# Zero rows only in the unused slots of a row buffer, and the places of rows worked out during the first batch of attention

## The reference

```python
# 1: attention, 16 heads, Dh = 32. Masked scores are zero, not minus infinity
scores = einsum('bthd,bshd->bhts', x @ Wq, x @ Wk) * tril(ones(T, T))
attn = softmax(scores / T ** 0.5, axis=-1)
x = layernorm(x + einsum('bhts,bshd->bthd', attn, x @ Wv) @ Wo)

# 2: routing over 4 experts by token id; ctx_2048[e] serves as Wg, Wu and Wd
expert = min(clip(token_ids, 0, 24999) // 6250, 3)
for e in range(4):
    y = (silu(x @ W[e].T) * (x @ W[e].T)) @ W[e].T
    out = where(expert == e, y, out)
x = layernorm(x + out)

# 3: gated feed-forward, of each 4 neighbours in h only the 2 largest are kept
h = silu(x @ w_gate) * (x @ w_up)
x = layernorm(x + sparsify_2to4(h) @ w_down)
```

## Time and profile before

| | us |
|---|---|
| median of 3 runs | 1153.69 |
| the profiled execution | 1154.83 |
| its span, first to last instruction | 1153.0 |
| TensorE busy in it | 1046.8 (91%) |
| VectorE busy | 749.7 (65%) |
| ScalarE busy | 479.6 (42%) |
| GpSimd busy | 278.7 (24%) |
| mean granted TensorE clock | 0.980 of full |

### The profile page before, as it was taken

One profiled execution on the slowest core, in us unless ns is written; L12 is line 12 of the kernel. 1 busy time (PEld: TensorE's weight loads), 2 busy tenths in 40 slices (PEclk: granted clock), 3 DMA queues, 4 the chain that ended last, 5 costly groups with the idle time before them and its releaser, 6 DMA issues.

```text
span 1153.0 us, 18006 instructions
## 1 busy us (share of the span) xinstructions
PE 1046.8 (91%) x6022; PEld 846.7 (73%) x6023; DVE 749.7 (65%) x1756; ACT 479.6 (42%) x882; POOL 278.7 (24%) x479
## 2 busy tenths in 40 slices
PE   2888999898999977499999999999999999999994
PEld 1666777776777766388788888888888888888873
DVE  4668768868886897365664845664565546654666
ACT  4268648856874895122333322221121222222113
POOL 1017444733653453122221002400000000000222
PEclk9999999999999998799999999999999999999997
DMA  5797725754672590122444101410010101100001
GB/s 182 187 303 214 188 87 153 198 128 143 176 196 55 147 274 11 64 84 81 149 164 165 37 1 22 53 38 1 1 44 29 36 0 36 37 1 1 38 37 73
DMA packets 56223, 110.37 MB, mean 96 GB/s; under 512 B 6032, under 2 KB 6032, under 8 KB 56144
## 3 DMA queue, kind: packets, MB, share of 16 engines
q1 hardware_dynamic: 51504, 95.97, 29.6%
q0 software_dynamic: 4640, 13.39, 3.1%
HBM read 72.11 MB, written 35.14 MB: 93 GB/s over the span
## 4 chain that ended last, share of the span: by engine, by line
PE 56%; DVE 2%; ACT 0%; issue 0%; POOLq 0%; POOL 0%; ACTq 0%; DVEq 0%
PE f_bank L42 54%; PE f_bank L1388 1%; PE f_bank L1380 1%; PE f_bank L1430 1%; DVE rows_kept L1727 0%; DVE ln_stats L813 0%; DVE big_hi L1108 0%; DVE hs_lo L1715 0%; DVE ln_mv L815 0%; ACT L826 0%; POOLq L1174 0%; DVE h L1705 0%; ACT hs_hi L1557 0%; POOL out L1342 0%; DVE ln_shift L833 0%
## 5 line engine op out<-in xcount | busy, mean ns | idle before, releaser
L1666 DVE TENSOR_TENSOR h<-f_bank,fsg 128x512 f32<-128x512 f32 x64 | 44.2, 691 | 181.9 <-PE f_bank L42 181.8
L1534 ACT ACTIVATE fsg<-f_bank 128x512 f32<-128x512 f32 x64 | 38.3, 599 | 298.4 <-PE f_bank L42 298.3
L404 PE MATMUL bank<-ident,probs 128*128 128x128 f32 x640 | 109.5, 286 | 37.9 <-DVE pt_lo L674 18.6
L654 DVE CUSTOM_DVE_ANT_0 bank<-bank,mask 128x384 f32<-128x384 f32 (+3 forms) x256 | 123.1, 503 | 24.3 <-PE bank L393 23.9
L531 ACT ACTIVATE probs<-bank,nmax 128x384 f32<-128x384 f32 (+3 forms) x256 | 129.7, 539 | 18.3 <-DVE nmax L665 16.4
L674 DVE TENSOR_TENSOR pt_lo<-bank,pt_hi 128x512 f16<-128x512 f32 (+1 forms) x192 | 114.7, 597 | 20.4 <-ACT pt_hi L541 20.0
L42 PE MATMUL bank<-x_hi,w_qk 128*128 128x512 f32 x256 | 104.9, 418 | 23.0 <-DVE x_lo L679 22.6
L844 POOL TENSOR_SCALAR ln_var<-ln_mv 128x1 f32<-128x1 f32 x43 | 10.0, 232 | 464.1 <-DVE ln_mv L815 464.1
L541 ACT ACTIVATE pt_hi<-bank 128x512 f16<-128x512 f32 (+1 forms) x192 | 102.9, 536 | 35.1 <-PE bank L404 34.3
L404 PEld LDWEIGHTS bank<-ident,probs 128*128 128x128 f32 x640 | 67.4, 141 | 49.2 <-ACT probs L531 28.1
L42 PE MATMUL f_bank<-wd_hi,hs_hi 128*128 128x512 f32 x256 | 100.3, 392 | 3.2 <-DVE rows_kept L1727 3.2
(11 more groups left out here) (225 smaller groups left out, 2438.5 us busy)
## 6 DMA issues: line engine op xcount, KB each, us to landing
big_lo<-q_hi_dram SPq DMA_DIRECT2D x32, 256.0 KB, 3.9
big_lo<-q_lo_dram SPq DMA_DIRECT2D x32, 256.0 KB, 4.7
big_lo<-k_hi_dram SPq DMA_DIRECT2D x32, 256.0 KB, 3.8
big_lo<-k_lo_dram SPq DMA_DIRECT2D x32, 256.0 KB, 5.2
sorted_dram<-z SPq DMA_DIRECT2D x1, 4864.0 KB, 18.7
rows<-sorted_dram SPq DMA_DIRECT2D x19, 256.0 KB, 2.6
x_raw<-x_t SPq DMA_DIRECT2D x4, 1024.0 KB, 9.9
q_hi_dram<-q_hi SPq DMA_DIRECT2D x16, 256.0 KB, 2.3
```

The source lines that it names most:

```text
L404: ins = pe.transpose(TP[u % TR][:, j * P:(j + 1) * P], probs[u % RP][:, j * P:(j + 1) * P], ident[:, :])
L654: dve.tensor_tensor_reduce(out=S[u % SR][:, at:at + cols(r)], in0=S[u % SR][:, at:at + cols(r)], in1=mask[:, T - cols(r):T], scale=1.0, sc ...
L1534: act.activation(fsg[v % 2][:, :], GB[v % 2][:, :], ACT.Silu).then_inc(s_sg, 1)
L1666: dve.tensor_tensor(h[r % 2][:, j, :], UB[v % 2][:, :], fsg[v % 2][:, :], ALU.mult).then_inc(s_h, 1)
```

## The change

The DMA that zeroes the whole row buffer goes, with its semaphores. In its place GpSimd scatters a tile of zeros (`z[0]`) three times, 128 rows each, to the 384 unused slots, after its `norm_heads` of group m = 2 in batch 0. `add_x` of batch 0 waits for these three. The numbers of the unused slots are worked out by 8 new VectorE instructions inside `Route.places` (one sum, three products and three sums, and the cast to `pad_idx`), and `places` now runs in batch 0 at every unit from 1 on, 31 instructions, instead of at every second unit of batch 3. `slot_f` is made earlier in the list.

```diff
@@ -103,7 +103,7 @@
         den2 = sb("den2", [P, NB, HEADS], F32)
         rinv = sb("rinv", [P, NB, HEADS], F32)
         z = [sb(f"z{i}", [P, D], F32) for i in range(NB)]
-        s_sc, s_zeroed = sem("s_sc"), sem("s_zeroed")
+        s_sc, s_pad = sem("s_sc"), sem("s_pad")
         ln = LayerNorm(nc, ctx, "ln1", D)
         bank = [ctx.enter_context(nc.psum_tensor(f"bank{i}", [P, 512], F32)) for i in range(8)]
 
@@ -116,9 +116,7 @@
 
         s_const = sem("s_const")
 
-        s_passed, s_passed_sp = sem("s_passed"), sem("s_passed_sp")
-        s_zero = sem("s_zero")
-
+        s_passed, s_passed_sp, s_passed_pool = sem("s_passed"), sem("s_passed_sp"), sem("s_passed_pool")
         s_xh = sem("s_xh")
         s_xl = sem("s_xl")
 
@@ -281,8 +279,6 @@
             pool.affine_select(out=mask[:, T - P:T], in_=mask[:, T - P:T], compare_op=ALU.is_ge, fill=0.0,
                                base=0, pattern=[[-1, P]], channel_multiplier=1).then_inc(s_const, 1)
 
-            pool.wait_ge(s_zero, 16)
-            pool.sem_inc(s_zeroed, 1)
             pool.wait_ge(route.s_idx_all, 1)
             for b in range(B):
                 more = b < B - 1
@@ -297,6 +293,11 @@
                                 x_lo(b + 1, k)
                     if m < NM - 1:
                         norm_heads(pool, 0, b, m)
+                    if b == 0 and m == NM - 2:
+                        wait_apart(pool, s_passed_pool, [(route.s_place, route.PAD_DONE)])
+                        for i in range(route.PADS):
+                            pool.indirect_dma_start(sorted_rows, bass.IndirectOffsetOnAxis(route.pad_idx[:, i:i + 1], 0),
+                                                    z[0][:, :], None).then_inc(s_pad, 16)
                 if more:
                     for j in range(NB):
                         v_last(b + 1, j)
@@ -357,10 +358,6 @@
             for g in range(G_AHEAD):
                 stack_up(0, g)
 
-            sp.wait_ge(s_const, NCONST)
-            tiles = sorted_rows.rearrange("(t p) d -> p t d", p=P)
-            zeros = z[0][:, :].unsqueeze(1).broadcast_to([P, sorted_rows.shape[0] // P, D])
-            sp.dma_start(tiles, zeros).then_inc(s_zero, 16)
             for b in range(B):
                 batch(b, b < B - 1)
 
@@ -716,7 +713,7 @@
                 dve.wait_ge(s_xres, (b + 1) * 16)
 
                 if b == 0:
-                    dve.wait_ge(s_zeroed, 1)
+                    dve.wait_ge(s_pad, route.PADS * 16)
                 else:
                     dve.wait_ge(s_sc, b * NB * 16)
                 dve.tensor_tensor(z[r][:, :], WB[r % 2][:, :], x_res[:, r, :], ALU.add).then_inc(s_z, 1)
@@ -727,9 +724,9 @@
                 ln.scale(dve, z[r], z[r], b * NB + r, r, s_x1)
 
             def batch(b, more):
-                places = route.places(dve) if not more else None
+                places = route.places(dve) if b == 0 else iter(())
                 for u in range(0 if b > 0 else -AHEAD_MAX, UPB - AHEAD_LO):
-                    if not more and u > 0 and u % 2 == 0:
+                    if u > 0:
                         next(places, None)
                     fresh = u + AHEAD_MAX < UPB and (b == 0 or u + AHEAD_MAX >= AHEAD_S)
                     if fresh:
@@ -903,6 +900,11 @@
         self.s_tok, self.s_c, self.s_v, self.s_m = [ctx.enter_context(nc.semaphore(n))
                                                     for n in ("s_tok", "s_rc", "s_rv", "s_rm")]
         self.N_ONEHOT = 3 + 2 * E + 1
+        self.PADS = NS - NT
+        self.PAD_DONE = 2 + E + 2 * (E - 1) + 2
+        self.pad_idx = sb("pad_idx", [P, self.PADS], I32)
+        self.pad_at = sb("pad_at", [P, self.PADS])
+        self.pad_over = sb("pad_over", [P, E - 1, self.PADS])
 
         self.s_idx_all = ctx.enter_context(nc.semaphore("s_idx_all"))
 
@@ -1012,13 +1014,27 @@
             yield
         did(ready().tensor_tensor(gap[:, :], base[:, :], first[:, :], ALU.subtract))
         yield
+        did(ready().tensor_copy(self.slot_f[:, :], self.slot_i[:, :]))
+        yield
+
+
+        unused = self.slot_f[:, 0:self.PADS]
+        did(ready().tensor_scalar(self.pad_at[:, :], unused, per[:, 0:1], None, ALU.add))
+        yield
+        for e in range(1, E):
+            did(ready().tensor_scalar(self.pad_over[:, e - 1, :], unused, gap[:, e:e + 1], per[:, e:e + 1], ALU.is_ge,
+                                      ALU.mult))
+            yield
+            did(ready().tensor_tensor(self.pad_at[:, :], self.pad_at[:, :], self.pad_over[:, e - 1, :], ALU.add))
+            yield
+        did(ready().tensor_copy(self.pad_idx[:, :], self.pad_at[:, :]))
+        assert count[0] == self.PAD_DONE
+        yield
         did(ready().tensor_tensor(stop[:, :], base[:, :], per, ALU.add))
         yield
         did(ready().tensor_tensor(self.gap_step[:, 1:E], gap[:, 1:E], gap[:, 0:E - 1], ALU.subtract))
         yield
         did(ready().tensor_tensor(self.stop_step[:, 1:E], stop[:, 1:E], stop[:, 0:E - 1], ALU.subtract))
-        yield
-        did(ready().tensor_copy(self.slot_f[:, :], self.slot_i[:, :]))
         yield
         for acc, by, start in ((shift, self.gap_step, gap), (end, self.stop_step, stop)):
             did(ready().tensor_scalar(acc[:, :], past[:, 0, :], by[:, 1:2], start[:, 0:1], ALU.mult, ALU.add))
```

## The result

| | before | after |
|---|---|---|
| median, 20 runs each | 1155.31 us | 1151.71 us |
| lowest to highest | 1152.78 to 1158.34 | 1150.08 to 1153.76 |
| profiled execution, span | 1154.83, 1153.0 us | 1151.63, 1149.8 us |
| mean granted clock | 0.980 | 0.979 |

The ratio is 0.9968 with a 95% interval of [0.996, 0.9977]: the change saves 3.6 us (2.7 to 4.6), where 5.9 were forecast. The time is inside the range of 1144.6 to 1152.0 and 3.9 us above the forecast of 1147.8. Of these 3.9, 1.6 are the base: 20 runs put the kernel before at 1155.31, and I had hung the number on three runs with a median of 1153.69. The other 2.3 are the change. (A ratio here is a kernel's time over that of the kernel before, run beside it; the brackets hold its 95% interval.)

What follows compares the result with a forecast made beforehand. TensorE, busy for 91% of the span, was held in batch 0 by a chain of waits from the zeroing; the terms gave -5.9 us, 1148.9 from the profile, 1147.8 against the runs' median, range 1144.6 to 1152.0.

Steps and rivals of the forecast that it cites:

- Term 1: Batch 0, heads 1 to 3: without the zeroing, TensorE's stall through GpSimd and ScalarE goes, -5.1 us.
- what is late next: SP's queue in batch 0: group-4 stacking, 12.6 us after the write behind the zeros, gets earlier too; whole 5.13 us taken.
- Term 2: VectorE in batch 0: 31 `places` instructions, mostly covered by its idle time, cost +0.4 us.
- Term 3: VectorE in batch 3: 23 instructions leave, which shortens the heads behind head 5, -1.2 us.
- Term 4: GpSimd: three scatters take 4.2 us, inside 4.8 us of slack before ScalarE's copy of head 14, 0 us.
- Rival (d): Scatters hold GpSimd over 4.8 us, so ScalarE waits again at head 14; 1147.9 us by rows; chance 0.04.
- The sum: Whole kernel: -5.1 + 0.4 - 1.2 + 0 = -5.9 us, from the profiled 1154.83 to 1148.9 us.
- (a): Between batches 0 and 1: the low-clock stretch may be gone, a further -1.6 us, 1146.2 us; chance 0.16.
- (b): VectorE's instructions half uncovered in batch 0, nothing back in batch 3: -1.6 us, 1152.1 us; chance 0.12.
- (c): Batch 0: only the direct wait goes, -3.7 us, and the next head stays long; 1149.2 us; chance 0.10.
- (e): Batch 0: all 31 VectorE instructions on the path, nothing back in batch 3; +1.9 us, 1155.6 us; chance 0.03.
- (f): GpSimd's first sums come as late as before, held by another condition; left at nothing.

Runs made afterwards that it cites:

- two spacer forms: The kernel before with an unused tile of 128 (s1_spacer) or 64 (u4_spacer64) bytes a partition in attention; 1156.99 us and 1154.9 us.
- u4_spacer64: The kernel before with one unused tile of 64 bytes a partition in attention; 1154.9 us in its single run.
- s2_home: The changed kernel with its three new tiles allocated behind attention's, so all others keep their old addresses; 1151.36 us, ratio 0.9967.
- v1_zero_late: The kernel before, zeroing issued behind the stacking of group 8, `add_x` of batch 0 waiting for it instead of GpSimd; 1153.0 us, ratio 0.9972.
- s1_spacer: The kernel before with one unused tile of 128 bytes a partition where the change has its new tiles; 1156.99 us, ratio 1.0013.
- u3_tuned: s2_home with one unused tile of 128 bytes a partition in front of `hs` in the late part; 1149.36 us, ratio 0.9959.
- s5_rest_late: s2_home with the first 14 `places` instructions in batch 0, the other 17 at even units of batch 3; 1151.21 us, ratio 0.9967.

## Why the prediction was right or wrong

**Term 1, the stall: -5.1 forecast, -4.4 to -5.1 measured.** The place, the mechanism and "what is late next" were right: both chains had to be freed, and the change frees both. The reading of 5.13 us was right for that execution (15.09 to 10.06 us). But what counts is when batch 0 ends. Over the seven profiles with the change's scatters copy 15 starts at 132.02 us in the mean; over the three of the kernel before at 136.92, over these and the two spacer forms at 136.26. These differences, -4.9 and -4.2, hold term 2, which is +0.2. The zeroes land at a time of their own, so if the first heads are late, before absorbs it, and after passes it on: in u4_spacer64 head 0 is at 66.75 and yet head 15 comes earliest of the profiles with the early zeroing, whose zeroes were issued earliest there (57.06 us, elsewhere 57.33 to 58.32). The stall of before is a meeting with a transfer, and its size changes with the execution.

**Term 2, VectorE in batch 0: +0.4 forecast, +0.2 measured** (0.17 us in heads 0 to 5, and 52.61 against 52.47 for heads 3 to 15, a little of it the addresses'). Right, near the lower end as argued.

**Term 3, batch 3: -1.2 forecast, -0.88 measured.** The sentence "at 3.80 the eight would take 30.4" was too good: they take 30.95, 3.87 a head, with ScalarE at 29.29 of it. The mechanism held, and the size was 0.3 us too large.

**Term 4, the scatters: 0 forecast, 0 measured.** Rival (d) fell: the longest scatter is 1.23 us, with VectorE busy for 3.0 of the 3.8 us of the three.

**The sum: the step that failed.** "-5.1 + 0.4 - 1.2 + 0" counts instructions and waits only, and puts every stretch whose instructions don't change at nothing, without a reason. The change also puts 128 bytes of SBUF in front of other tiles, and in the traces that costs 3 x 0.31 us between batches and 0.07 in each of batches 1 and 2: +1.1 us. With it the sum is between -4.9 + 1.1 - 0.9 = -4.7 and -4.2 + 1.1 - 0.9 = -4.0. The measured -3.6 [-4.6, -2.7] agrees with the lower saving and just excludes the higher. So of the 2.3 us that are missing 1.1 are the addresses and 0.3 is term 3, term 2 gives 0.2 back, term 1 is between 0 and 0.7, and 0.4 to 1.1 us have no cause that is shown.

A part of it stands behind attention. In the three profiles of before the last copy of batch 3 starts at 439.91 us in the mean, in the two of after at 433.80: 6.1 us earlier, even with the addresses' cost (0.7 of it is the mean of the stretch between batches 0 and 1, where the clock was lower in two of the three). The tail of the same profiles is 1.8 us longer. That the long tail belongs to the changed kernel isn't shown, and its cause is open. Nor is the +1.1 us shown in the medians: by the same sum s2_home, without it, should save 5.1 to 5.8 us, and its ratio says 3.8 [2.4, 5.1], no more than the changed kernel. The account has the sign and the places; against the medians it leaves 0.4 to 1.1 us open for the changed kernel and 1.3 to 2.0 for s2_home.

**The base.** "That execution stands 1.14 us above the median of the runs" was true of three runs. Against 20 it stands 0.5 below. With the mean effect as forecast I would still have been 1.6 us low. That the time fell into the range is partly the range's width: it was drawn around a base 1.6 us too low and an effect 2.3 us too large, and 1151.71 is 0.3 us inside its upper end. The prediction's 0.5% as the least that can be told from no change was too coarse: with 20 runs of each, 0.3% is told from none.

**Rivals.** (a) comes and goes between executions, of either kernel; in the profiles of before it was there in two of three, in those of after in neither. (b) fell in both halves: 0.2 us is uncovered in batch 0, not 3.5, and 0.9 comes back in batch 3. (c) and (e) have nothing for them: the second head is short again, and 0.2 us is uncovered, not over 5.1. (f) fell with the waits.

## What to carry to other kernels

Measure a stall by when the stage behind it ends, over several executions, and look for a second chain on the same transfer before crediting one wait: here taking away one of two gained nothing. A large fill on a queue that a pipeline uses belongs where no stacking follows soon; in v1_zero_late its place on the queue counted for more than its bytes. After a change that adds a tile, compare a stretch that it doesn't touch: if its matmuls have grown at the same clock, allocate the new tile behind the others. In the traces that gave back 0.3 us a stretch; in the medians it didn't show.

## What the runs showed of the hardware that I had not expected

- The address of a matmul's operands in SBUF shows in its pace. Matmuls of the same pair, with 512 columns at full granted clock, start 227.4 to 229.0 ns or 232.0 to 233.5 ns apart, by 64 or 128 bytes of unused tile in front (`x_hi` and `ot_hi` with `big_hi`, in s1_spacer and u4_spacer64; `gt_hi` and `xt_hi` with `big_hi` in u3_tuned). Other pairs moved by 0.5 to 3.8 ns. Why is open; I have only the distances of a few pairs modulo 256 bytes. The Trainium skill, SBUF — State Buffer, section "Operand start alignment", says of its own measurements that they concern legality and timed nothing.
- A zero fill of 4864 KB lands 18.2 us after its issue in v1_zero_late (17.5 to 18.7 us in the profiles with the early one), and a small DMA issued 3.5 us behind it on the same queue holds SP for 5.78 us instead of 0.34 (s5_rest_late).
- The stretch between batches 0 and 1 takes either 35.7 or 37.3 us, granted clock 1.00 or 0.95, in executions of one and the same program. The window of s2_home, in the form of the earlier trace rows:

```profile
132.63:169.90 37.27, 34.49 (x182) 27.14 (x181) 23.97 (x65) 16.31 (x30) 13.48 (x24) 0.95 0.38 110
```
